# Who empties the Q/K projection bank: the copies of pairs 1 to 7 moved from ScalarE to VectorE

## The chip, the cores and the metric

One Trainium2 chip, eight cores. Each core runs the same program on one sequence of the batch, and no core talks to another. The metric is device time in microseconds of the slowest core.

## What is computed

A transformer layer, post-norm, for 8 sequences of 2048 tokens, width 1024, 16 heads of 64, feed-forward width 4096:

```python
q, k, v = split(x @ w_qkv)               # 16 heads of 64
q, k = rope(q), rope(k)
a = softmax(causal(q @ k.T) * 64**-0.5) @ v
x = layernorm(x + a @ w_out)
# weights rounded to -1, 0, 1 times their mean magnitude, activations to 8 bits per row
x = layernorm(x + bitlinear(silu(bitlinear(x, w_gate)) * bitlinear(x, w_up), w_down))
```

## The kernel before

Every engine has a queue of its own (a `Lane`), filled by one Python program in one order. An engine runs its queue strictly in that order; a wait at its head holds all that stands behind. So where an instruction stands in an engine's queue is fixed by when the code issues it.

**Prologue.** The x, the V weights and the first Q/K weights are loaded and cast, the heads' pair 0 (heads 0 and 1) is projected to Q and K, and V is computed for all heads. Pairs are numbered 0 to 7, two heads each.

**Attention.** The loop at L1040 runs over 320 steps, 40 for each pair: query block j of 512 columns, key block kc of 128 rows, causal. In a step, in this order: two score matmuls into one of two double PSUM banks (`scores`, L621) and their exponential on ScalarE (L632), with a causal mask by GpSimd on the diagonal (L637); some items of `fill`; the PV matmuls and the sums for the step three back (`attend`, L654); `tick`, which runs what was put off with `later`; and background items (`bg_item`). The scores of step s wait for the exponential of step s-2.

**The fill.** While pair c is attended, the Q and K of later pairs are projected. `fill` is a list of 56 groups (7 pairs, K then Q, four column blocks each) of 8 items; an item is two 64-column matmuls over one block of the contraction (L401). All of these groups use one PSUM bank, `PJ`. The first item of a group waits until the bank is free (`pj_free`); behind the last item one copy takes the bank to SBUF in bf16 (L411). 1.6 items are issued per step (2.4 in pair 0), so a group takes about five steps, and after the last item of a group no item is issued in the next step (`skip`, L1059). From the fourth column block of K and of Q hangs the rotary embedding (`rope`, L420): 2 and 3 steps later GpSimd's queue issues transfers that swap halves into `swp`, and 11 steps later VectorE gets three instructions of 2048 columns (L431 to L433). GpSimd's causal masks are in the same queue as the swap transfers. The scores of a pair wait for its last rotary instruction.

**VectorE's other work in that time.** Background items, about 1.4 per group of the fill: `A`, a reduction of the magnitudes of a 1 MB weight tile (L497), or `B`, two instructions that quantize one (L521, L523); a cast of Q/K weights for each pair (L490); and the division by the softmax sum for each query block (L680), which is issued 4 steps after the block's end and waits for Ln and Exp on ScalarE (L674, L676). Three times a threshold is worked out, with a small matmul into `PJ` (L540) that waits for the bank and for a reduction on VectorE.

**After attention** come the output projection and the feed-forward part, which keep TensorE busy to the end.

Of the kernel before, what the change touches and what calls it, by code (L numbers as in the profile page):

```python
# [11 lines left out]
AF = mybir.ActivationFunctionType  # L12
# [98 lines left out]
def build_program():  # L111
# [22 lines left out]
    with es:  # L134
        def sem(name):
            return es.enter_context(nc.semaphore(name))

        pe = Lane(sem("pe"), False)
        act = Lane(sem("act"), True)
        dve = Lane(sem("dve"), True)  # L140
# [243 lines left out]
        qk_free = [None] * 3  # L384
# [3 lines left out]
        def proj_group(c, w, nb, bk="pj"):  # L388

            B = PJ if bk == "pj" else SU  # L390
            out = []
            for kc in range(8):
                def one(kc=kc):
                    toks = []
                    if kc == 0:
                        while c not in t_wqk:
                            bg_item()
                        toks = [t_wqk[c], t_x[(nb, 0)], t_x[(nb, 1)], pj_free[bk]]
                    cuts = ((0, 128),) if c == 0 else ((0, 64), (64, 128))
                    for a, z in cuts:  # L400
                        fn = lambda e, a=a, z=z: e.matmul(  # L401
                            B[a:z, :], wqk[c % 2][:, kc, w * 128 + a:w * 128 + z],
                            xT[:, kc, nb * 512:(nb + 1) * 512], start=(kc == 0), stop=(kc == 7))
                        if kc == 7 and z == 128:
                            t = pe.do(fn)
                        else:
                            pe.quiet(fn, *toks)
                    if kc < 7:
                        return
                    dst = QK[c % 3][w][:, nb * 512:(nb + 1) * 512]  # L410
                    t2 = act.do(lambda e: e.activation(dst, B, AF.Copy), t, qk_free[c % 3])  # L411
                    pj_free[bk] = t2
                    if w == 0 and nb == 3:
                        wqk_free[c % 2] = t
                    if nb == 3:
                        rope(c, w, t2)
                out.append(one)
            return out

        def rope(c, w, t2):  # L420
            X, W = QK[c % 3][w], swp[w]

            def swap(bs):
                for b in bs:
                    o = b ^ 1
                    pool.dma(s_sw[w], W[b * 32:(b + 1) * 32, :], X[o * 32:(o + 1) * 32, :], t2, swp_free[w])
                if bs[0]:
                    later(11 if c else 5, lambda: finish(s_sw[w].tok()))

            def finish(ts):  # L430
                r1 = dve.do(lambda e: e.tensor_tensor(W, W, sinT, ALU.mult), ts, t_tab)  # L431
                r2 = dve.do(lambda e: e.tensor_tensor(X, X, cosT, ALU.mult))
                r3 = dve.do(lambda e: e.tensor_tensor(X, X, W, ALU.add), r1, r2)  # L433
                swp_free[w] = r3
                t_rope[(c, w)] = r3
            later(1 if c == 0 else 2, lambda: swap((0, 1)))
            later(1 if c == 0 else 3, lambda: swap((2, 3)))
# [117 lines left out]
        for nb in range(4):  # L555
# [4 lines left out]
            for hf in range(2):  # L560
                for tq in range(4 * nb, 4 * nb + 4):
                    b = vn % 4
                    vn += 1
                    for kc in range(8):
# [8 lines left out]
                        else:  # L573
                            t = pe.do(fn)
                    dst = V[:, tq, hf * 512:(hf + 1) * 512]
# [464 lines left out]
        for s in range(nstep + LAG):  # L1040
            if s < nstep:
                c, j, kc = steps[s]
# [38 lines left out]
        for t in range(NT + LAGD):  # L1081
# [38 lines left out]
            else:  # L1120
                B = DN if (t - NT) % 2 else G
# [88 lines left out]
```

How the kernel before makes its waits and increments, by code:

```python
    def emit(self, eng):  # L85
        for fn, want, sem, k in self.q:
            last = None
            if self.embed and want:
                last = want[-1]
                want = want[:-1]
            for s, v in want:
                eng.wait_ge(s, v)
            ins = fn(eng)
            if last is not None:
                ins.wait_op(last[0], last[1], "sem-ge")
            if sem is not None:
                ins.then_inc(sem, k)
# [1038 lines left out]
        @block.sync  # L1136
        def _(e):
            sp.emit(e)
            for sl in s_out:
                if sl.n:
                    e.wait_ge(sl.sem, sl.n)
```

## Time and profile before

| | us |
|---|---|
| median of 3 runs | 1225.07 (1224.86 lowest) |
| the profiled execution | 1223.76 |
| its span, slowest core (core 2) | 1222.2 |
| spans of the eight cores | 1214.8 to 1222.2 |
| granted TensorE clock, mean | 0.988 to 0.993 |

One execution was profiled on every core; all rows are of core 2. Times in a trace count from the first instruction of the program. The busy time of an engine leaves out waits; a matmul's end is modelled. A row of the timeline may stand for several neighbouring instructions, then it has their number behind an x.

### The profile page before, as it was taken

The page shows a single profiled execution, that of the slowest core. Times are in us where ns is not written, and L with a number is a line of the kernel's source. Part 1 is how long each engine was busy: PE and PEld are TensorE (multiplying, and loading weights), DVE is VectorE, ACT ScalarE, POOL GpSimd, SP SyncE. Part 2 cuts the span into 40 slices and gives each one's busy share as a digit, 9 for nine tenths or more (in the row PEclk, how much of TensorE's full clock was granted, in tenths as well). Part 3 has the DMA queues.
Part 4 walks back from the last instruction along what each step waited for, and adds up shares of the span by engine and source line. Part 5 has one row for each costly group of instructions (what it writes and reads, how often), then busy time and mean ns, then how long its engine had stood idle before and what let it go on. Part 6 is the DMA issues. An engine that isn't in the chain of part 4 may idle for free.

```text
span 1222.2 us, 17266 instructions; the slowest of 8 cores (1214.8 to 1222.2 us)
## 1 busy us (share of the span) xinstructions
PE 1157.6 (95%) x6470; PEld 493.4 (40%) x6470; DVE 701.5 (57%) x999; ACT 665.6 (54%) x847; POOL 125.0 (10%) x217
## 2 busy tenths in 40 slices
PE   3898999999999988999999999999999999999998
PEld 1343333333333322344444444444444444444443
DVE  2369866676676843478884544554544544543343
ACT  4236899998998987644445245235344344343400
POOL 3011134132332231000000000000000000000000
PEclk9998999999999999899999999999999999999999
DMA  9999999966999785457786344344344333332482
GB/s 281 314 322 335 271 283 321 306 215 180 287 325 316 254 277 156 146 158 220 224 206 147 95 119 115 78 121 121 75 120 116 78 95 112 69 99 74 103 161 73
DMA packets 152705, 225.22 MB, mean 184 GB/s; under 512 B 107888, under 2 KB 112112, under 8 KB 137264
## 3 DMA queue, kind: packets, MB, share of 16 engines
q1 hardware_dynamic: 148784, 214.28, 60.2%
q0 software_dynamic: 3840, 9.84, 2.8%
q8 instruction: 54, 0.88, 0.3%
q14 instruction: 27, 0.22, 0.1%
HBM read 148.19 MB, written 46.53 MB: 159 GB/s over the span
## 4 chain that ended last, share of the span: by engine, by line
PE 76%; ACT 12%; DMA 6%; POOL 3%; DVE 1%; issue 1%; DVEq 0%; SPq 0%; ACTq 0%
PE sc L851 36%; PE av L915 16%; ACT E L632 9%; PE pj L401 6%; PE sc L621 5%; PE pj L770 5%; DMA ring<-wg 4%; PE av L654 4%; PE su L654 3%; PE sc L915 2%; POOL E L637 2%; DMA ring<-xu 2%; ACT Rb L676 1%; ACT Lb L674 1%; ACT QK L411 1%
## 5 line engine op out<-in xcount | busy, mean ns | idle before, releaser
L632 ACT ACTIVATE E<-sc,cst 128x1024 bf16<-128x1024 f32 (+1 forms) x320 | 301.8, 987 | 42.3 <-PE sc L621 40.8
L861 ACT ACTIVATE sg<-sc,st 128x512 bf16<-128x512 f32 x128 | 87.8, 686 | 306.5 <-PE sc L851 285.8
L851 PE MATMUL sc<-TG,xqT 128*128 128x512 fp8e4 x1024 | 241.9, 379 | 0.0
L851 PE MATMUL sc<-TU,xqT 128*128 128x512 fp8e4 x1024 | 241.9, 379 | 0.0
L915 PE MATMUL av<-TD,hqT 128*128 128x512 fp8e4 x896 | 195.7, 379 | 0.0
L867 DVE TENSOR_TENSOR h<-sc,sg 128x512 f32<-128x512 f32 x128 | 88.3, 690 | 163.0 <-PE sc L851 140.9
L401 PE MATMUL pj<-xT,wqk 128*64 128x512 bf16 (+1 forms) x928 | 149.9, 400 | 23.2 <-DVE xT L354 20.9
L851 PEld LDWEIGHTS sc<-TG,xqT 128*128 128x128 bf16 x1024 | 100.2, 98 | 120.8
L851 PEld LDWEIGHTS sc<-TU,xqT 128*128 128x128 bf16 x1024 | 100.2, 98 | 120.8
L621 PE MATMUL sc<-QK,QK 64*128 64x512 bf16 (+3 forms) x640 | 117.2, 361 | 22.6 <-ACT E L632 19.1
L915 PEld LDWEIGHTS av<-TD,hqT 128*128 128x128 bf16 x896 | 87.7, 98 | 105.7
L654 PE MATMUL av<-E,V 128*64 128x512 bf16 (+3 forms) x640 | 118.4, 363 | 8.7 <-POOL E L637 8.3
L497 DVE TENSOR_REDUCE part<-ring 128x1 f32<-128x2048 f32 x48 | 107.9, 2279 | 18.2 <-DMA ring<-wg 15.0
L637 POOL TENSOR_SCALAR_AFFINE_SELECT E<-E 128x256 bf16<-128x256 bf16 x128 | 79.9, 634 | 313.0 <-ACT E L632 312.7
L654 PE MATMUL su<-E,onesb 128*64 128x512 bf16 (+3 forms) x640 | 110.0, 354 | 0.0
L886 ACT ACTIVATE hq<-h,cst,st 128x512 f16<-128x512 f32 x128 | 92.9, 799 | 18.5 <-DVE st L880 18.5
L871 DVE TENSOR_REDUCE st<-h 128x1 f32<-128x512 f32 x128 | 87.9, 686 | 4.4
L621 PEld LDWEIGHTS sc<-QK,QK 64*128 64x128 bf16 x640 | 32.6, 93 | 139.8 <-issue 137.4
L940 DVE SCALAR_TENSOR_TENSOR y<-av,dsc,yr 128x512 f32<-128x512 f32 x28 | 20.8, 743 | 105.3 <-PE av L915 102.9
L401 PEld LDWEIGHTS pj<-xT,wqk 128*64 128x64 bf16 (+1 forms) x928 | 47.5, 109 | 83.1 <-issue 66.0
L680 DVE TENSOR_TENSOR ao<-av,Rb 128x512 bf16<-128x512 f32 x32 | 22.1, 690 | 85.8 <-ACT Rb L676 85.8
L770 PE MATMUL pj<-wo,aot 128*128 128x512 bf16 x256 | 61.2, 379 | 0.3 <-DVE y L780 0.2
(87 smaller groups left out, 887.2 us busy)
## 6 DMA issues: line engine op xcount, KB each, us to landing
ring<-wg SPq DMA_DIRECT2D x28, 1024.0 KB, 19.4
ring<-wu SPq DMA_DIRECT2D x28, 1024.0 KB, 11.9
ring<-wd SPq DMA_DIRECT2D x16, 1024.0 KB, 8.4
dstg<-wd SPq DMA_DIRECT2D x16, 1024.0 KB, 7.0
hqs<-hq SPq DMA_DIRECT2D x64, 256.0 KB, 2.7
ring<-wqk SPq DMA_DIRECT2D x8, 1024.0 KB, 12.8
ring<-xu SPq DMA_DIRECT2D x8, 1024.0 KB, 25.7
swp<-QK POOLq DMA_DIRECT2D x64, 128.0 KB, 8.3
```

The source lines that it names most:

```text
L401: fn = lambda e, a=a, z=z: e.matmul(B[a:z, :], wqk[c % 2][:, kc, w * 128 + a:w * 128 + z], xT[:, kc, nb * 512:(nb + 1) * 512], start=(kc = ...
L497: t = dve.do(lambda e: e.tensor_reduce(part[:, m, n:n + 1], ring[i], AXX, ALU.add, apply_absolute_value=True), tk)
L621: fn = lambda e, p0=p0, hh=hh: e.matmul(out[:, hh, lo:512], Kt[p0:p0 + 64, kc * 128:(kc + 1) * 128], Q[p0:p0 + 64, j * 512 + lo:(j + 1) * ...
L632: t2 = act.do(lambda e: e.activation(Et[:, :, lo:512], out[:, :, lo:512], AF.Exp, bias=c_(4), scale=0.125), t, *more)
L637: t2 = pool.do(lambda e: e.affine_select(tri, tri, [[0, 2], [1, 128]], ALU.is_ge, 0.0, base=0, channel_multiplier=-1), t2)
L654: fn = lambda e, hh=hh, w=w, dst=dst, q=q, lq=lq, kq=kq: e.matmul(dst, w, E[q % NE][:, hh, lq:512], start=kq == 0, stop=sp_ and q == s)
L770: fn = lambda e, c=c: e.matmul(OP, aot[p][:, c, :], wo[:, c, hf * 512:(hf + 1) * 512], start=(c == 0), stop=(c == 7))
L851: fn = lambda e, kc=kc, dst=dst, W=W: e.matmul(dst, x_[:, kc, :], W[:, n, kc * 512:(kc + 1) * 512], start=(kc == 0), stop=(kc == 7))
L867: c = dve.do(lambda e: e.tensor_tensor(h[:, n, :], U[b], sg[b], ALU.mult), tm, a, h_free[n])
L871: t_h2[n] = dve.do(lambda e: e.tensor_reduce(col(t, 21 + n), h[:, n, :], AXX, ALU.max, apply_absolute_value=True), c)
L886: t_hq[n] = act.do(lambda e, n=n: e.activation(hq[:, n, :], h[:, n, :], AF.Identity, bias=c_(6), scale=col(t, 32)), t_hqs[t], hq_free[n])
L915: fn = lambda e, kc=kc, hf=hf: e.matmul(banks_[hf], hqT[:, kc, :], TD[:, kc, hf * 512:(hf + 1) * 512], start=(kc == 0), stop=(kc == 31))
```

## The change

In `proj_group` the copy behind a group of pair 0 stays on ScalarE, and the copies of pairs 1 to 7 are issued on VectorE, at the same place of the code and with the same waits:

```diff
                     dst = QK[c % 3][w][:, nb * 512:(nb + 1) * 512]
-                    t2 = act.do(lambda e: e.activation(dst, B, AF.Copy), t, qk_free[c % 3])
+                    if c == 0:
+                        t2 = act.do(lambda e: e.activation(dst, B, AF.Copy), t, qk_free[c % 3])
+                    else:
+                        t2 = dve.do(lambda e: e.tensor_copy(dst, B), t, qk_free[c % 3])
                     pj_free[bk] = t2
                     if w == 0 and nb == 3:
                         wqk_free[c % 2] = t
```

`t` is the group's last matmul. `t2` is what the next group's first matmul waits for, and after the fourth column block what the swap transfers wait for. Nothing else changes.

## Rows read from the trace of the kernel before

**Rows 1.** The page's head and part 1: busy us, share, instructions.

```profile
span 1222.2 us, 17266 instructions; the slowest of 8 cores (1214.8 to 1222.2 us)
PE 1157.6 (95%) x6470; PEld 493.4 (40%) x6470; DVE 701.5 (57%) x999; ACT 665.6 (54%) x847; POOL 125.0 (10%) x217
```

**Rows 2.** Stages: stretch, length, busy PE, PEld, DVE, ACT, POOL; clock, DMA, GB/s.

```profile
100.00:431.00 331.00, 309.56 (x2446) 119.36 (x2448) 238.31 (x184) 295.66 (x369) 94.80 (x156) 0.98 0.88 277
431.00:504.00 73.00, 60.83 (x390) 18.91 (x386) 24.01 (x38) 62.68 (x76) 15.85 (x28) 0.93 0.61 197
```

**Rows 3.** Waits, 100 to 431 us: engine, line, releaser: total us, times, longest.

```profile
PE sc L621 <- ACT E L632: 11.4, 18, 1.3
PE av L654 <- POOL E L637: 5.0, 8, 1.0
PE pj L540 <- ACT QK L411: 2.4, 2, 1.5
DVE ao L680 <- ACT Rb L676: 56.1, 19, 7.3
```

**Rows 4.** VectorE's groups by form, 100 to 431 us: count, busy, mean ns, idle before.

```profile
L497 DVE TENSOR_REDUCE part<-ring 128x1 f32<-128x2048 f32 x40 | 89.6, 2277 | 5.0 <-DMA ring<-wu 3.3 <-DMA ring<-wg 1.8
L521 DVE TENSOR_SCALAR cmp<-ring,wsc 128x2048 fp8e4<-128x2048 f32 x32 | 42.1, 1315 | 0.0
L523 DVE TENSOR_SCALAR f8o<-cmp 128x2048 fp8e4<-128x2048 fp8e4 x32 | 40.0, 1249 | 3.1
L431 DVE TENSOR_TENSOR swp<-swp,sinT 128x2048 bf16<-128x2048 bf16 x13 | 16.2, 1244 | 17.3 <-DMA swp<-QK 17.3
```

**Rows 5.** The copies of pairs 1 to 7, L411: min/median/max ns, first and last.

```profile
L411 ACT ACTIVATE QK<-pj x56: 587/588/613, 103.8 to 430.8; 128x512 bf16<-128x512 f32 x56
```

**Rows 6.** Groups by form, whole span: VectorE's nearest to the new copy.

```profile
L780 DVE TENSOR_TENSOR y<-pj,xt 128x512 f32<-128x512 f32 x32 | 22.0, 689 | 9.3 <-PE pj L770 9.0 <-issue 0.3
L330 DVE TENSOR_SCALAR tbb<-tb 128x512 bf16<-128x512 f32 x1 | 0.4, 429 | 0.0
```

**Rows 7.** Timeline, pair 2, sixth to eighth group: start, us, engine, line, what.

```profile
167.48 0.41 PE L401 MATMUL pj<-xT,wqk 128*64 128x512 bf16 x2
...
171.24 1.23 DVE L431 TENSOR_TENSOR swp<-swp,sinT 128x2048 bf16<-128x2048 bf16 x1 [2.60 <-DMA swp<-QK]
...
172.78 0.41 PE L401 MATMUL pj<-xT,wqk 128*64 128x512 bf16 x2
...
176.08 1.05 PE L401 MATMUL pj<-xT,wqk 128*64 128x512 bf16 x8
176.16 1.23 DVE L523 TENSOR_SCALAR f8o<-cmp 128x2048 fp8e4<-128x2048 fp8e4 x1
```

**Rows 8.** Timeline, start of attention, VectorE and TensorE.

```profile
97.74 15.44 DVE L497 TENSOR_REDUCE part<-ring 128x1 f32<-128x2048 f32 x7
...
103.08 0.64 PE L401 MATMUL pj<-xT,wqk 128*64 128x512 bf16 x2
...
106.36 1.74 PE L401 MATMUL pj<-xT,wqk 128*64 128x512 bf16 x12
```

**Rows 9.** Short stretches; the last column but two is the granted clock.

```profile
98.00:103.00 5.00, 3.66 (x22) 1.11 (x22) 5.00 (x3) 3.77 (x4) 1.22 (x3) 0.71 1.00 354
103.00:107.00 4.00, 4.00 (x20) 1.12 (x20) 4.00 (x3) 2.71 (x4) 0.41 (x1) 0.51 1.01 324
...
270.00:276.00 6.00, 4.86 (x40) 2.04 (x40) 5.76 (x5) 5.91 (x9) 0.00 (x0) 1.00 0.07 25
282.00:288.00 6.00, 4.53 (x40) 1.83 (x36) 1.73 (x4) 3.96 (x6) 1.89 (x5) 0.98 0.46 157
288.00:292.00 4.00, 4.00 (x22) 1.18 (x20) 3.65 (x3) 3.10 (x4) 0.00 (x0) 0.60 0.15 20
```

**Rows 10.** Timeline, end of pair 1's rotary embedding and its first scores.

```profile
149.72 1.22 DVE L433 TENSOR_TENSOR QK<-QK,swp 128x2048 bf16<-128x2048 bf16 x1
...
155.31 0.39 PE L621 MATMUL sc<-QK,QK 64*128 64x512 bf16 x2
```

## The prediction, before the run

> **What bounds the kernel now.** I read the page first [rows 1]: TensorE is busy for 1157.6 of 1222.2 us, VectorE for 57% and ScalarE for 54% of the span. Those are means over stages, so the next view was the table of busy time by stage [rows 2]. All 56 copies that the change touches run between 103.8 and 430.8 us [rows 5]. In that stretch (100 to 431 us) TensorE is busy for 309.6 of 331 us, ScalarE for 295.7 (89%), VectorE for 238.3 (72%). TensorE and ScalarE are both nearly full, and TensorE is the fuller: it is idle for 21.4 us, ScalarE for 35.3. From 431 to 504 us ScalarE has the exponentials almost alone, with no projection left, and after 504 us TensorE does the feed-forward part; the change touches neither.
>
> The waits of the stretch [rows 3] say what TensorE's 21.4 idle us are: 11.4 for an exponential, 5.0 for GpSimd's causal mask, 2.4 for a copy ahead of a threshold matmul; 0.8 more for a copy stands in the listing of L401's waits. So ScalarE costs TensorE at most 11.4 + 2.4 + 0.8 = 14.6 us here, which caps the gain. The last row of [rows 3] matters as much: VectorE sits 56.1 us at the head of its queue waiting for the 1/sum of a block. It runs ahead of the others in its own program and stops only there. Its spare time is therefore time in which it is early, and what it does early are long instructions [rows 4]: reductions of 2.28 us, quantizing pairs of 1.32 + 1.25 us, rotary threes of about 3.7 us.
>
> **The change part by part.** Removed from ScalarE: 56 x 0.588 = 32.9 us [rows 5]. TensorE gets back only what it waited for. Six of its waits on exponentials are of 1.05 us, in the seventh group of pairs 2 to 7, behind Ln and Exp of a block end and not behind a copy; one of 1.26 is the first step's table load. That leaves 11.4 - 6.3 - 1.3 = 3.8 us, and with the 0.8 some 4.6; I take 3.7 us of gain. The threshold's 2.4 stays: that matmul will wait for VectorE's copy and its small reduction instead.
>
> Added to VectorE: 56 copies. The trace has no such copy. The nearest rows read 512 fp32 columns from PSUM in 0.69 us [rows 6]; the second row there is a 512-column fp32 to bf16 instruction from SBUF, 0.43 us. I take 0.69, because its source is PSUM, and keep 0.43 as the bound. 56 x 0.69 = 38.6 us makes VectorE 277 of 331 us busy, 84%: enough room on average. The Trainium skill, "VectorE: DVE Perf Modes", section on the TRN2 errata, gives 120 + 512 cycles at 0.96 GHz for PSUM to SBUF, estimated 0.66 us; by it the 14 stalls below would be 0.4 us shorter together.
>
> The average is not what decides. There is one PSUM bank PJ for the projection groups, and the next group's first matmul stands in TensorE's in-order queue behind the copy (L399 to L411). I call ge the end of a group's last matmul and the window the time from there to the next group's first matmul; it is 1.4 to 1.6 us for most groups and 2.89 for the seventh of pairs 2 to 7. On ScalarE the copy had only the current exponential in front. On VectorE it has all that the code issued between the previous copy and itself, and VectorE can no longer take that early, because the previous copy waits for TensorE. So
>
> copy done = later of (ge + 0.05) and (previous copy done + work queued between) + 0.69, and TensorE goes on 0.14 us after it.
>
> I went through the 56 groups in the code's order, each queued instruction at its duration less 0.08 us of overlap with the next (seven reductions take 15.44 us and not 16.0 [rows 8]), waits for transfers kept where the trace has them. What comes out:
>
> - Start of attention. Seven reductions from 97.74 to 113.18 us are queued around the first of these copies, the sixth ending at 110.98; the group ended at 103.7 and the next began at 106.36 [rows 8]. Copy from 110.98, done 111.67, TensorE at 111.81: 5.45 us lost.
> - The seventh group of pairs 2 to 7. Queued before it are the rotary three and up to two quantizing pairs or reductions, 7.4 to 8.9 us. In pair 2 [rows 7]: the sixth group ended at 167.89, its copy would be done at 168.6, the queued seven instructions take 8.92 - 0.56 = 8.36, the copy 0.69, TensorE at 177.8 instead of 176.08: 1.7 us. A check that needs no model: VectorE ended that queued work at 177.39 even though it ran ahead (the last row), so 178.2. The six give 1.77, 1.58, 1.70, 1.65, 1.71 and 1.24 = 9.65 us.
> - Groups with a rotary three and one more pair, 5.9 to 6.9 us of work in an interval of about 6, or right behind a late copy: seven small stalls from 0.01 to 0.98 us, in all 2.95 us.
>
> Sum 18.05 us. All other groups have 2 to 5 us of work in about 6 us and lose nothing. Without early running counted at all (only ends of queued work as they stand in the trace) it is 12.6 us; with no overlap deducted 23.0. These are the two bounds.
>
> The rotary three of pair 1 is late too: it ended at 150.94 and the pair's first scores ran at 155.31 [rows 10]. Behind the copy of the third group (done 151.9) its queue takes 5.8 us: 157.6, a wait of 2.3 us on TensorE, of which 1.0 is in the list already: +1.3. At the later boundaries the rotary three ends several steps ahead of the first scores, and behind the last group of all nothing is queued but reductions.
>
> TensorE's clock. After the stretch in which it was busy for 3.66 of 5 us it was granted 0.51 to 0.71, and after 4.53 of 6 us (a single 1.47 us wait for a copy) 0.60; where it was busy for 4.86 of 6 it stayed at 1.00 [rows 9]. The levels are 2.4 and 1.2 GHz, and 4 us at 0.60 is 3.2 us at half speed, 1.6 us lost. A seventh group will have 1.05 + 1.7 us idle close together, more than either. I count four more such dips out of eight possible places, 4 x 1.7 = 6.8 us; bounds one and eight, 1.7 and 13.6.
>
> Sum: +18.05 + 1.3 + 6.8 - 3.7 = +22.5 us. The profiled span is 1222.2, so 1244.7; the profiled run 1223.8 us, so 1246.3; on the median of 1225.07 it is 1247.6. Forecast 1248 us. No transfer is added: the swap transfers hang on the copy and have 11 steps until they are used.
>
> **The rivals.**
> A, the forecast: VectorE's queue order costs TensorE some 20 us. 1229 to 1263 with its bounds.
> B, the other side: the copies keep up. The one mechanism is that queued work between two copies fits into interval plus window. It holds if the seventh groups have less than 8.19 - 0.83 - 0.74 = 6.6 us queued; they have 7.4 to 8.9, and at the start 7.3 us of lateness stand in the trace. Then 3.7 to 14.6 us come back: 1210 to 1221. Speaking for it: VectorE 72% busy.
> C, it cancels: copies near 0.43 us, stalls at 12.6 - 3.6 = 9 us, no dips, ScalarE giving back up to 14.6: 1221 to 1234.
> D, lateness spreads: GpSimd's queue issues the swaps once the copy is done, and its causal masks stand behind. A late fourth or eighth group then also delays masks and PV matmuls, 13 places at about 1 us, with all eight dips: 1263 to 1280. Against it: only one of those groups is late in my list, by 1.6 us.
>
> The Trainium skill, "Perfetto Trace Analysis", section on Scalar/DVE operations, advises moving work off VectorE if that one is saturated, and breaking up instructions where engines that are not saturated still make bubbles elsewhere. By its first half this move is harmless at 72 to 84% and would end as B, at 1210 to 1221 us; by its second half it is the 2.28 us instructions that count, which [rows 8] bear out.
>
> **How the numbers follow.** A 0.66, B 0.07, C 0.12, D 0.15. A difference under 2% (24.5 us) is about what a measurement of this kernel can't tell from no change: the border is 1249.6. A lies across it, 0.39 below and 0.27 above; B and C are within, D beyond. Faster 0.01, within 2% 0.57, slower 0.42. The range leaves out B, a little of C and half of D: 1229 to 1268.
>
> **What would show it.** Right: a wait of TensorE L401 on VectorE's copy, some 15 to 20 us in all, the longest 5 us near 106 us and about 1.7 us once a pair; ScalarE's busy time 33 us lower with more idle time on scores; VectorE's wait for 1/sum falling from 56 to under 20 us, because it waits at the copies; the projections ending some 20 us later. Wrong: TensorE's waits for VectorE under 8 us (then B or C), masks or PV matmuls late by over 15 us (D), or a copy of 0.43 us. If the waits are there and the time is not, the clock term or ScalarE's gain was mis-sized.

## The result: 2.5% slower

The changed kernel takes 1254.74 us (median of four runs, 1254.01 to 1257.11) beside 1224.99 us before: ratio 1.0254, 95% interval 1.0241 to 1.0267. The forecast was 1248 us in a range of 1229 to 1268, with a chance of 0.42 on slower by over 2%; the likelier outcome by its chances, a change within 2% (0.57), did not come. Ratios and intervals, here and below, are of the runs in the fast state alone, so they can differ by 0.1% from the quotient of the medians: by the ratio the change costs 31 us of 1225, and the runs below are counted against that.

I read core 2 in both kernels, since the rows of before are of that core; its span grew from 1222.2 to 1251.2 us. First the waits of the stretch with the projections (98 to 460 us, which answers to [rows 3]): engine, line, releaser, total us, times, longest. A line number of after is 3 higher than before wherever it stands below the edit, and some of the later runs shift it by a few more. A view marks lines left out with `...`.

```profile
ACT E L635 <- PE sc L624: 81.8, 89, 9.8
DVE QK L414 <- PE pj L401: 74.5, 32, 5.2
...
PE pj L401 <- DVE QK L414: 18.4, 9, 7.2
PE av L657 <- POOL E L640: 11.3, 9, 2.7
DVE ao L683 <- ACT Rb L679: 9.7, 8, 2.6
PE sc L624 <- ACT E L635: 7.8, 12, 1.1
...
PE sc L624 <- DVE QK L436: 3.4, 1, 3.4
...
PE pj L543 <- DVE tiny L542: 1.5, 2, 1.0
```

TensorE waited 18.4 us for VectorE's copies, in nine places. VectorE's early running is gone: instead of 56.1 us at the 1/sum [rows 3] it waits 9.7 us there and 74.5 us at the copies. It still has spare time, and the spare time still cannot be used where it is needed. ScalarE, which was to be relieved, now waits 81.8 us for scores (31.5 us before).

The new copy itself costs what its nearest rows cost ([rows 6] and the seven-tenths of a microsecond there); the page of the changed kernel, which is of core 5, has it as

```profile
L414 DVE CAST QK<-pj 128x512 bf16<-128x512 f32 x56 | 38.5, 688 | 77.9 <-PE pj L401 77.7
```

The stretch by the table of stages, columns as in [rows 2], first before, then after:

```profile
98.00:430.00 332.00, 310.33 (x2452) 119.54 (x2454) 240.17 (x184) 296.10 (x369) 94.80 (x156) 0.98 0.88 279
```

```profile
98.00:460.00 362.00, 318.50 (x2444) 119.25 (x2444) 269.14 (x237) 271.16 (x313) 96.93 (x156) 0.94 0.80 253
```

TensorE's idle time grew from 21.7 to 43.5 us, and its granted clock fell from 0.98 to 0.94. The second window misses eight matmuls at its start. From the first scores (98.1 us before, 96.3 after) to the last projection (430.1 and 460.3) both kernels have 2452 matmuls, and TensorE is busy for 310.4 and 320.5 us. This stretch grew by 32 us; the parts before and after it gave back 3, of which 1.7 are the earlier first scores, ahead of any changed instruction.

Three places of it. First the start of attention, which answers to [rows 8], in the timeline of after (start, us, engine, line):

```profile
96.00 13.24 DVE L500 TENSOR_REDUCE part<-ring 128x1 f32<-128x2048 f32 x6
...
100.87 0.41 PE L401 MATMUL pj<-xT,wqk 128*64 128x512 bf16 x2
109.16 0.68 DVE L414 CAST QK<-pj 128x512 bf16<-128x512 f32 x1
...
109.99 0.64 PE L401 MATMUL pj<-xT,wqk 128*64 128x512 bf16 x2 [7.19 <-DVE QK L414]
```

The group was done at 101.3 us. Its copy began 7.9 us later, behind six reductions, and TensorE stood still for 7.19 us, from 102.8 us on.

Next the seventh group of pair 2, which answers to [rows 7]:

```profile
181.06 1.23 DVE L434 TENSOR_TENSOR swp<-swp,sinT 128x2048 bf16<-128x2048 bf16 x1
...
182.59 0.41 PE L401 MATMUL pj<-xT,wqk 128*64 128x512 bf16 x2
183.46 1.22 DVE L436 TENSOR_TENSOR QK<-QK,swp 128x2048 bf16<-128x2048 bf16 x1
184.60 1.28 DVE L524 TENSOR_SCALAR cmp<-ring,wsc 128x2048 fp8e4<-128x2048 f32 x1
185.99 1.23 DVE L526 TENSOR_SCALAR f8o<-cmp 128x2048 fp8e4<-128x2048 fp8e4 x1
187.13 0.68 DVE L414 CAST QK<-pj 128x512 bf16<-128x512 f32 x1
...
187.96 1.05 PE L401 MATMUL pj<-xT,wqk 128*64 128x512 bf16 x8 [2.17 <-DVE QK L414]
```

The group ended at 183.0; the rotary three and a quantizing pair went first. And the place that the forecast did not have, the end of pair 2's projection beside the diagonal of a block:

```profile
221.41 1.42 DVE L524 TENSOR_SCALAR cmp<-ring,wsc 128x2048 fp8e4<-128x2048 f32 x1
221.70 2.57 POOL L74 DMA_DIRECT2D swp<-QK  x2
...
222.94 1.24 DVE L526 TENSOR_SCALAR f8o<-cmp 128x2048 fp8e4<-128x2048 fp8e4 x1
224.28 0.42 POOL L640 TENSOR_SCALAR_AFFINE_SELECT E<-E 128x256 bf16<-128x256 bf16 x1
224.63 1.97 POOL L74 DMA_DIRECT2D swp<-QK  x2
224.84 0.30 PE L657 MATMUL av<-E,V 128*64 128x256 bf16 x2 [1.49 <-POOL E L640]
226.61 0.42 POOL L640 TENSOR_SCALAR_AFFINE_SELECT E<-E 128x256 bf16<-128x256 bf16 x1
227.17 0.32 PE L657 MATMUL av<-E,V 128*64 128x128 bf16 x2 [1.60 <-POOL E L640]
```

Two issues of swap transfers hold GpSimd for 2.57 us while VectorE quantizes; the mask of 0.42 us stands behind them, and TensorE behind the mask. The next two issues take 1.97 us, with the same end. Three places of this kind, near 225, 333 and 387 us, hold 10.3 of the 11.3 us of waits on masks. At the same place of the kernel before, VectorE was done with its pairs and the first two issues took 0.99 us. The next two took 1.74 us there too, and the mask behind them cost TensorE 1.02 us:

```profile
208.42 0.99 POOL L74 DMA_DIRECT2D swp<-QK  x2
209.42 0.42 POOL L637 TENSOR_SCALAR_AFFINE_SELECT E<-E 128x256 bf16<-128x256 bf16 x1
209.77 1.74 POOL L74 DMA_DIRECT2D swp<-QK  x2
```

### The profile page after: what moved, and what is told of

Read it like the earlier page. It is cut to its first block, busy times and chain, and to the rows that moved or that the text cites. A ratio compares the mean times of both kernels' runs of the same rounds, so it can differ in the third digit from the quotient of the medians.

```text
span 1252.2 us, 17243 instructions; the slowest of 8 cores (1245.6 to 1252.2 us)
## 1 busy us (share of the span) xinstructions
PE 1168.6 (93%) x6470; PEld 494.3 (39%) x6470; DVE 735.0 (59%) x1055; ACT 641.9 (51%) x791; POOL 128.7 (10%) x217
## 4 chain that ended last, share of the span: by engine, by line
PE 76%; DMA 7%; ACT 6%; DVE 6%; POOL 4%; issue 1%; DVEq 0%; SPq 0%; ACTq 0%
PE sc L854 35%; PE av L918 15%; PE pj L401 7%; ACT E L635 5%; PE sc L624 5%; PE pj L773 5%; DMA ring<-wg 4%; PE av L657 4%; PE su L657 3%; POOL E L640 2%; PE sc L918 2%; DMA ring<-xu 2%; POOL swp L74 2%; DVE part L500 1%; DMA swp<-QK 1%
## 5 line engine op out<-in xcount | busy, mean ns | idle before, releaser
L401 PE MATMUL pj<-xT,wqk 128*64 128x512 bf16 (+1 forms) x928 | 153.9, 412 | 37.9 <-DVE xT L354 19.2
L500 DVE TENSOR_REDUCE part<-ring 128x1 f32<-128x2048 f32 x48 | 108.7, 2277 | 12.4 <-DMA ring<-wg 12.4
L414 DVE CAST QK<-pj 128x512 bf16<-128x512 f32 x56 | 38.5, 688 | 77.9 <-PE pj L401 77.7
```

The source lines that it names most:

```text
L401: fn = lambda e, a=a, z=z: e.matmul(B[a:z, :], wqk[c % 2][:, kc, w * 128 + a:w * 128 + z], xT[:, kc, nb * 512:(nb + 1) * 512], start=(kc = ...
L500: t = dve.do(lambda e: e.tensor_reduce(part[:, m, n:n + 1], ring[i], AXX, ALU.add, apply_absolute_value=True), tk)
```

## The experiments

The theory: a copy costs TensorE what stands ahead of it in VectorE's queue (queue order). Rivals: every copy on VectorE costs about the same; GpSimd's masks are the main loss; and, for the gain, that ScalarE really bounds the stretch.

**1. The seven latest copies back on ScalarE.**

```diff
-                    if c == 0:
+                    if c == 0 or (c, w, nb) == (1, 1, 0) or (c > 1 and (w, nb) == (0, 2)):
                         t2 = act.do(...)
```

> As the changed kernel, but 7 of the 56 moved copies stay on ScalarE: the first one (pair 1, first group) and the seventh group of pairs 2 to 7, those with the most VectorE work queued ahead. Queue-order theory (a copy costs TensorE only what stands ahead of it on VectorE): the waits of TensorE on these copies, about 16 of 18.4 us, go, and with them 4 to 6 stretches at half clock, so 18 to 24 us less than the changed kernel: about 1233 us. Rival that each copy on VectorE costs about the same: 7/56 of 29.7 us, so 1251 us. Rival that GpSimd's masks are the main loss: 1250 us or more.

Measured: 1241.51 us, ratio 1.0149 (1.0124 to 1.0173). Thirteen of the 31 us are gone with an eighth of the copies, which neither equal cost nor the masks as the main loss gives, but I had expected some 22. Its waits (slowest core, 98 to 460 us) say why:

```profile
PE av L657 <- POOL E L640: 11.3, 10, 2.7
...
PE pj L401 <- DVE QK L414: 7.2, 4, 3.9
...
PE sc L624 <- DVE QK L436: 3.5, 1, 3.5
```

The waits on the seventh groups are gone. At the start the wait moved to the second group, 3.9 us, because the six reductions stand there too. Masks and pair 1's rotary embedding are as late as before: they don't hang on the seven copies.

**2. No copy at all.** The copies of pairs 1 to 7 are left out and Q and K of these pairs are zeros, so attention computes on other values.

```diff
-                        t2 = dve.do(lambda e: e.tensor_copy(dst, B), t, qk_free[c % 3])
+                        t2 = t
```

> The copies of pairs 1 to 7 are left out altogether (Q and K of these pairs are zeros, so attention works on other values); the next group waits for nothing and neither ScalarE nor VectorE does the work. It measures what the relief of ScalarE is worth by itself. From the waits in the trace of before (3.8 us on exponentials, 2.4 and 0.8 on copies) some 5 to 8 us less than before: 1217 to 1220 us. The rival that ScalarE bounds the stretch and that its 33 us come back for the most part: 1195 to 1205 us.

Measured: 1215.09 us, ratio 0.9931 (0.9912 to 0.9950). This is 2 us below the range that I had expected (1217 to 1220) and far from the 1195 to 1205 of the rival. So ScalarE's 33 us of copies were worth 8 to 9 us in all, the waits on the bank included. This caps every placement of them while the swap transfers stay in GpSimd's queue.

**3. Only the seven on VectorE.**

```diff
-                    if c == 0:
+                    if not ((c, w, nb) == (1, 1, 0) or (c > 1 and (w, nb) == (0, 2))):
                         t2 = act.do(...)
```

> The complement of the first run: only those 7 copies on VectorE, the 49 others on ScalarE. VectorE can again run ahead between them. Queue-order theory: the lateness that stands in the trace of before, 5.5 us at the start and some 6 us over the six seventh groups, plus 2 to 5 stretches at half clock: 12 to 20 us more than before, 1237 to 1245 us. Rival of equal cost for each copy: 1229 us.

Measured: 1239.11 us, ratio 1.0124 (1.0105 to 1.0144): 15 us for seven copies, as the queue order had it. TensorE's waits on them are 11.2 us (slowest core), 5.3 of them at the start; the masks' are small here:

```profile
DVE ao L683 <- ACT Rb L679: 75.7, 20, 8.5
...
PE pj L401 <- DVE QK L414: 11.2, 5, 5.3
...
PE av L657 <- POOL E L640: 2.7, 6, 0.6
```

VectorE runs ahead again (75.7 us at the 1/sum), and with that the masks' waits are 2.7 and not 11.3 us. The waits on masks come with VectorE being held back, not with late copies.

**4. Swap transfers from SyncE's queue, all pairs.**

```diff
-                    pool.dma(s_sw[w], ...)
+                    sp.dma(s_sw[w], ...)
```

> As the changed kernel, but the rotary swap transfers are issued from SyncE's queue instead of GpSimd's, so that no causal mask stands behind one. If TensorE's 11.3 us of waits on masks come from the swap issues ahead of them, these fall to 3 to 5 us and the time by 6 to 9 us, to about 1247 us. If they come from the masks themselves running slowly beside VectorE's instructions, the waits stay at 8 to 11 us and the time at 1252 to 1255 us. Side effect to watch: SyncE then holds the weight loads while it waits for a copy, which could cost some us.

Measured: 1250.70 us, ratio 1.0221 (1.0201 to 1.0241). The waits on masks fell to 1.8 us, but the time was 4 us above the 1247 expected, and the side effect came too: with pair 0's swaps behind SyncE's loads the first scores ran at 102.4 us instead of 96.3 (core 2). So it was done again without that.

**5. The same for pairs 1 to 7 only, and on the kernel before.**

```diff
-                    pool.dma(s_sw[w], ...)
+                    (sp if c else pool).dma(slot, ...)     # slot: a semaphore of its own for SyncE
```

> The changed kernel, with the swap transfers of pairs 1 to 7 issued by SyncE and those of pair 0 by GpSimd as before. Beside the earlier run in which all were SyncE's and the start of attention came 5 us late. If the masks' 11.3 us of waits are worth their size, 1244 to 1248 us; if other waits take their place, 1250 us or more.

Measured: 1243.42 us, ratio 1.0170 (1.0151 to 1.0188) against the kernel before, where the changed kernel has 1.0254: 10 us less. Waits of core 2, 98 to 450 us:

```profile
PE pj L402 <- DVE QK L415: 18.0, 8, 7.3
...
PE sc L627 <- DVE QK L439: 3.5, 1, 3.5
...
PE av L660 <- POOL E L643: 1.8, 3, 0.6
```

The waits on copies are nearly untouched at 18.0; the masks' went from 11.3 to 1.8, although single masks still take up to 1.39 us there. So those waits came mainly from the swap issues ahead of the masks, and not from slow masks. On the kernel before the same edit does nothing:

> The kernel before, with the swap transfers of pairs 1 to 7 issued by SyncE. It tells how much of a gain of the run beside it is due to the swaps alone. TensorE's waits on masks are 5.0 us in the kernel before; if the issue ahead of the mask is their cause they fall to 1 to 2 us: 1220 to 1223 us. If SyncE's waits hold up the weight loads: 1225 to 1230 us.

Measured: 1222.99 beside 1222.49 us, ratio 1.0001 (0.9991 to 1.0010). There, on core 2 from 98 to 430 us, the masks' waits fell from 5.0 to 0.2 us, but the waits on exponentials rose from 11.4 to 13.9 and those ahead of the threshold matmuls from 2.4 to 4.4: others took their place.

**6. Half the background work.** All 56 copies on VectorE; each reduction and quantizing pair but the first four pairs works on half its columns, and the rest of the weights is left out.

```diff
-    tensor_reduce(part[:, m, n:n + 1], ring[i], ...)
+    tensor_reduce(part[:, m, n:n + 1], ring[i][:, 0:UN // 2], ...)
```

> The changed kernel with all 56 copies on VectorE, but every background instruction (reduction, quantizing pair) works on half of its columns, the first four pairs excepted; the other half of the weights is left out. Same instructions, same order, about 1.2 instead of 2.3 to 2.6 us for each item. Queue-order theory: nearly all waits on copies go (below 3 us), with the lateness of pair 1 and the clock's stretches: 1218 to 1226 us. Rival that a copy from PSUM on VectorE is costly whatever stands before it: above 1240 us.

Measured: 1228.13 us, ratio 1.0042 (1.0028 to 1.0056). The 56 copies from PSUM are all there and 26 of the 31 us are gone, so their own cost is not the bulk of it. But the masks' waits are gone as well (0.4 us up to the last projection), so the run does not part the two losses. It is 2 us above what I expected, and the waits on copies, expected below 3 us, are 7.7 us on core 2 and 12.4 on the slowest core. What is left, from the timeline of core 2 and its waits:

```profile
105.62 1.22 DVE L500 TENSOR_REDUCE part<-ring 128x1 f32<-128x1024 f32 x1 [2.06 <-DMA ring<-wg]
106.75 0.68 DVE L414 CAST QK<-pj 128x512 bf16<-128x512 f32 x1
107.58 2.77 PE L401 MATMUL pj<-xT,wqk 128*64 128x512 bf16 x12 [5.61 <-DVE QK L414]
...
PE sc L625 <- DVE QK L436: 3.5, 1, 3.5
```

With short reductions the start is hardly better, 5.61 instead of 7.19 us: VectorE then waits for the weight tiles (2.06 us twice), and the copy waits with it. Of the other waits on VectorE, 1.44 us at the copy before 149 us and the 3.5 us above, before 163 us, lie where the four pairs of full size stand (144 to 167 us); one of 0.61 us lies at 376 us.

**7. The copies placed by what is queued ahead, and swaps on SyncE.** 38 copies on VectorE, 18 on ScalarE: those that the prediction's walk through the queue found late, and those with a rotary three or the start's reductions right behind or ahead. The swap transfers of pairs 1 to 7 go to SyncE by the edit of run 5, not shown again here.

```diff
-                    if c == 0:
+                    late = {1: (0, 1, 2), 2: (0, 2, 3, 4, 6)}.get(c, (2, 6))
+                    if c == 0 or (1 - w) * 4 + nb in late:
                         t2 = act.do(...)
```

> 38 of the 56 copies on VectorE, those that have little queued ahead; 18 stay on ScalarE: first to third group of pair 1, groups 1, 3, 4, 5, 7 of pair 2, groups 3 and 7 of pairs 3 to 7. The swap transfers of pairs 1 to 7 are issued by SyncE, so no mask stands behind them. Queue-order theory: waits on VectorE's copies below 2 us, masks below 2 us, and two thirds of the 9 us that the relief of ScalarE is worth: 1214 to 1221 us. Rival that holding VectorE back from running ahead costs by itself, wherever the copies stand: 1228 to 1238 us.

Measured: 1215.26 beside 1222.49 us, ratio 0.9939 (0.9926 to 0.9951): 7 us below the kernel before, clear of the noise though far under 2%. That is about what run 2 gained; as the swaps moved too, run 2 is no cap for it. Waits of core 2, 98 to 450 us:

```profile
PE sc L628 <- ACT E L639: 13.6, 25, 1.1
...
PE av L661 <- POOL E L644: 2.4, 4, 0.6
PE pj L547 <- DVE tiny L546: 2.4, 2, 1.4
...
PE pj L402 <- ACT QK L414: 0.2, 1, 0.2
```

No projection matmul (L402 here) waits for a VectorE copy in the answer. The last projection ends at 417.5 us here; up to there the waits on exponentials are 9.4 us, beside 11.4 before, and TensorE is busy for 305.5 us, beside 310.4. With the swaps left to GpSimd:

> The mended kernel (38 copies on VectorE, 18 with much queued ahead on ScalarE), but with the swap transfers issued by GpSimd as in the kernel before. It parts the two edits of the mended one. If the placement alone gives the gain, 1214 to 1217 us. If VectorE, held at its copies, still puts its background work beside the swap issues and the masks, as in the changed kernel, TensorE waits 8 to 11 us on masks and the time is 1222 to 1230 us. I expect the second.

Measured: 1230.83 beside 1226.13 us, ratio 1.0040 (1.0026 to 1.0054), with

```profile
PE av L658 <- POOL E L641: 12.1, 10, 2.7
```

on core 2. The two edits together, as ratios to the kernel before:

| copies of pairs 1 to 7 | swaps by GpSimd | swaps by SyncE (pairs 1 to 7) |
|---|---|---|
| all on ScalarE | 1 | 1.0001 |
| 38 of 56 on VectorE, by queue | 1.0040 | 0.9939 |
| all on VectorE | 1.0254 | 1.0170 |

Moving the swaps is worth nothing while the copies are on ScalarE and 10 to 12 us (0.84 and 1.01% of 1225) once copies hold VectorE back.

## Why the prediction was right, and what it missed

The terms of the sum, in us, core 2:

| term | forecast | measured |
|---|---|---|
| waits on VectorE's copies | +18.05 | +18.4 |
| pair 1's rotary three | +1.3 | +3.4 |
| TensorE's clock | +6.8 | +10.1 of busy time |
| waits on exponentials, and on ScalarE's copies in the bank | -3.7 | 11.4 to 7.8 and 0.8 to 0: -4.4 |
| threshold matmuls | 0 | 2.4 to 1.5: -0.9 |
| waits on masks | 0 | 5.0 to 11.3: +6.3 |
| sum | +22.5 | +32.9 |

The stretch itself grew by 31.9 us and the span by 29.0. So the mechanism was right, and the total came out low mainly for the masks.

**The queue's walk held.** Of the 14 places, the start was forecast at 5.45 us and took 7.19: the first group was done 2.4 us earlier than in the kernel before and the sixth reduction only 1.7, and TensorE had other work for 1.5 us behind the group instead of 2.6. The seventh groups of pairs 2 to 7 were forecast at 1.77, 1.58, 1.70, 1.65, 1.71 and 1.24 and took 2.17, 1.66, 1.29, 0.86, 1.99 and 1.30, 9.27 for 9.65 in all. The total of the six was met, the single places only to 0.8 us. Of the seven small ones two came (1.44 and 0.54 us for 2.95 in all). Runs 1 and 3 bear the mechanism out from two sides, seven copies moved back and seven alone; run 6, the work ahead halved, agrees.

**The rotary three of pair 1** held the scores for 3.45 us where I had 2.3, of which 1.0 was counted as stalls behind it. Those stalls did not come; the wait at the scores took their place. That term was mis-sized by 2 us.

**The gain of ScalarE** was -4.4 in waits, for 3.7 forecast. Run 2 says that without any other cost it would be 8 to 9 us, some 5 above what I took. Of the waits, the six of 1.05 us and the masks' stayed, as I had assumed: run 2 still has 8.6 us on exponentials and 5.5 on masks up to its last projection (core 2). What I had put at nothing is TensorE's busy time: it falls from 310.4 to 304.3 us on core 2, at a granted clock of 0.99 instead of 0.98, and by 2.7 to 6.6 us on cores 0, 5 and 7. Run 2 works on zeros; run 7, with the true values, shows the same (305.5 us).

**The step that was missing** is the masks. The forecast had them in rival D only, by a late fourth or eighth group holding up the swap issue, and set against it that only one of these groups is late. That was true and not the point. The swap issues came at their time but took 2.57 us for two instead of 0.99, beside quantizing pairs that VectorE had done earlier in the kernel before. I had noted that VectorE's early running ends, and had drawn from it only what it does to the copies, not what its long instructions would then lie beside. Run 5 measures what it is worth: 9.5 us of waits on masks go, and 10 us of time with them, where the same edit on the kernel before gains nothing. The 6.3 us of added waits alone would have made the forecast 1254, the 10 us 1258, 3 above what was measured.

**The clock** was counted with four more stretches at half speed. Around the waits of the changed kernel, columns as in [rows 9]:

```profile
107.00:111.00 4.00, 1.01 (x6) 0.61 (x8) 4.00 (x4) 0.00 (x0) 0.00 (x0) 0.50 0.94 340
...
186.00:189.00 3.00, 1.04 (x10) 0.73 (x12) 3.00 (x4) 1.26 (x2) 0.00 (x0) 0.99 0.66 169
189.00:193.00 4.00, 4.00 (x22) 1.02 (x18) 1.83 (x2) 1.46 (x2) 0.00 (x0) 0.58 0.80 287
222.00:228.00 6.00, 2.91 (x24) 1.03 (x21) 4.39 (x5) 3.77 (x5) 5.01 (x6) 0.87 0.94 281
228.00:232.00 4.00, 4.00 (x20) 1.40 (x20) 0.69 (x1) 2.87 (x4) 0.00 (x0) 0.50 1.03 319
```

After each of the two places at 186 and 222 us the 2.4 GHz fall to 1.2 for most of the next 4 us. Over the stretch TensorE's busy time grew by 10.1 us, of which the masks' places have a share. Run 5, without them, has 3.2 us more than before on core 2 and 6.6 to 7.1 more on cores 0, 5 and 7, so 6.8 was within what the copies alone cost. Which place falls was not foreseen: the forecast took the two idle times of a seventh group as the sign, but the granted clock stayed at 1.00 behind 1.05 and 1.99 us of waiting near 405 us (404 to 412). Why one place falls and another does not, no run here shows.

**The rule of the Trainium skill** that was named beside rival B ("Perfetto Trace Analysis", Scalar/DVE operations) came out by its second half: VectorE was not saturated (269 of 362 us) and made bubbles, and run 6, which shortens its instructions by leaving half of the work out, took more than half of them away (18.4 to 7.7 us on core 2). That splitting them without leaving work out would help was not tried; I doubt it, because the sum queued ahead of a copy stays the same.

**The 2%** that the forecast called the limit of what a measurement can tell is no more than a border between its classes: the interval here is 1.0241 to 1.0267, and that of run 7 lies below 1 at a change of 0.6%. Two ends of its ranges do not follow from its terms either: the lower bounds of A, 12.6, 1.3 and 1.7 us, give 1226 less ScalarE's whole 14.6 and 1237 less 3.7, not 1229, and C's 9 less 14.6 gives 1219 to 1220, not 1221. The measured time lies far from both.

## What to carry to other kernels

Before moving an instruction that another engine waits for to an engine "with a third of its time free", list what its queue holds between this instruction and the one before it, and set that sum against the time until the result is needed: VectorE was 74% busy, enough on average, and its order cost 18 us at nine places. An engine that runs ahead is not idle but early, and instructions that tie it to the others end this for all the rest, which then lies beside other work (here 6 us more of waits on masks, and 10 us of time by run 5). Moved copy by copy, by what is queued ahead, and with the queue cleared that the rest would collide with, the same idea gained 0.6%.

## What the runs showed that I had not expected

GpSimd's instructions are long only beside certain instructions of VectorE. One issue of a swap transfer takes 0.49 us at least, and up to 1.53 in the changed kernel; a mask takes 0.40 to 0.42 us, and up to 1.49:

```profile
L74 POOL DMA_DIRECT2D swp<-QK x52: 489/505/1529, 124.2 to 437.6; - x52
...
L640 POOL TENSOR_SCALAR_AFFINE_SELECT E<-E x104: 401/407/1486, 99.3 to 446.0; 128x256 bf16<-128x256 bf16 x104
```

(instructions on one line or tile, min/median/max ns, core 2). The kernel before has such long ones too (up to 1.34 and 1.44 us); what is new is where they fall. In the rows of both kernels that show a GpSimd instruction by itself, every mask beside nothing, beside a reduction or beside a copy from PSUM takes 0.40 to 0.42 us (the reductions alone: 50 masks); the longer ones, 0.44 to 1.49 us, lie beside the quantizing pairs, the casts of Q/K weights and the rotary three. Issues are long beside quantizing pairs and casts, as at 221 us, and take 0.49 us beside reductions and, twice, beside the rotary three. The Trainium skill, "Perfetto Trace Analysis", section on Scalar/DVE operations, says that GpSimd and VectorE share a read port of SBUF, which some VectorE instructions hold alone; these rows fit it for the masks. No run here isolates the cause, for masks or for issues.

And a lateness in a queue can be a transfer's in disguise: with the reductions halved the first copy still came 5.6 us late, because the queue in front of it then waited for weight tiles.
